# Attention score units of two heads moved among the last chunk's query, key and value products

## What is computed

```python
xn = _layernorm(x, axis=-1)
# attention
qkv = jnp.einsum('bnc,dc->bnd', xn, qkv_w) + qkv_b        # 16 heads of 32
attn = jax.nn.softmax(jnp.einsum('bhqd,bhkd->bhqk', q, k) * scale, axis=-1)
out = jnp.einsum('bhqk,bhkd->bhqd', attn, v)              # then proj_w, proj_b
# feed-forward, two picked experts of each batch
_, idx = jax.lax.top_k(xn[:, 0, :] @ Wr + br, 2)
h = jax.nn.gelu(jnp.einsum('bsd,bkde->bkse', xn, W1[idx]) + b1[idx], approximate=False)
o = jnp.einsum('bkse,bkef->bksf', h, W2[idx]) + b2[idx]   # mean over the two
x = x + attention + mean(o)
```

## Time and profile before

| | us |
|---|---|
| median of 3 runs | 4660.69 |
| lowest and highest run | 4658.37, 4661.96 |
| the profiled execution | 4660.65 |
| its span (first to last instruction) | 4658.9 |
| TensorE busy in the span | 4623.1 |
| VectorE, GpSimd, ScalarE busy | 3206.6, 3176.1, 2392.8 |

### The profile page before, as it was taken

The page is one execution under the profiler, slowest core; times in us unless marked ns, Lnnn a source line. Parts: engine busy times, 40 slices in busy tenths (PEclk is TensorE's granted clock), DMA queues, the critical chain, the costliest instruction groups (busy, mean ns, idle before and its releaser), DMA issues.

```text
span 4658.9 us, 65600 instructions
## 1 busy us (share of the span) xinstructions
PE 4623.1 (99%) x24396; PEld 2958.7 (64%) x24396; DVE 3206.6 (69%) x5313; ACT 2392.8 (51%) x4649; POOL 3176.1 (68%) x1105
## 2 busy tenths in 40 slices
PE   8999999999999999999999999999999999999999
PEld 7888888888755555555555555555555555555567
DVE  5233233333388888888888888888888888888854
ACT  2112121121146666666666666666666666666631
POOL 1121212121268999999999999999999999999910
PEclk9999999999999999999999999999999999999999
DMA  5334353434346666566666666665666666666557
GB/s 176 108 118 138 95 163 93 133 117 135 104 100 135 131 138 135 130 136 135 132 139 133 132 136 134 136 135 128 138 137 132 135 135 132 138 133 136 120 181 259
DMA packets 263425, 629.23 MB, mean 135 GB/s; under 512 B 46788, under 2 KB 83652, under 8 KB 224712
## 3 DMA queue, kind: packets, MB, share of 16 engines
q0 software_dynamic: 36288, 264.26, 27.9%
q1 hardware_dynamic: 226824, 360.85, 27.5%
HBM read 224.96 MB, written 134.74 MB: 77 GB/s over the span
## 4 chain that ended last, share of the span: by engine, by line
PE 62%; POOL 5%; DMA 3%; issue 2%; ACT 1%; DVE 0%; POOLq 0%; DVEq 0%
PE st_ps L1493 20%; PE o_ps L1419 18%; PE mx_ps L1407 18%; POOL p_pair L1121 4%; PE mx_ps L1433 3%; PE st_ps L1441 3%; DMA p_pair<-p_pair 3%; PE mx_ps L1441 1%; ACT p_sb L1197 1%; POOL p_pair L1159 0%; PE mx_ps L1412 0%; POOL o_inv L1115 0%; POOL p_pair L1125 0%; ACT front L1207 0%; DVE y_in L1286 0%
## 5 line engine op out<-in xcount | busy, mean ns | idle before, releaser
L1232 DVE TENSOR_REDUCE unit_max<-mx_ps 128x1 f32<-128x512 f32 x4016 | 2456.4, 682 | 311.1 <-PE mx_ps L1407 309.0
L1197 ACT ACTIVATE p_sb<-st_ps 128x512 f32<-128x512 f32 x4096 | 2063.3, 628 | 860.4 <-PE st_ps L1493 860.3
L1121 POOL TENSOR_TENSOR p_pair<-p_sb 128x2048 f32<-128x2048 f32 x504 | 2433.5, 4875 | 6.7 <-PE mx_ps L1433 3.4
L1419 PE MATMUL o_ps<-p_sb,v_sb 128*32 128x512 f32 x8192 | 986.7, 599 | 0.0
L358 POOL TENSOR_TENSOR h_lo<-h_f,h_hi 128x512 fp32r<-128x512 f32 x128 | 165.3, 1291 | 709.1 <-DVE h_hi L576 709.1
L1419 PEld LDWEIGHTS o_ps<-p_sb,v_sb 128*32 128x32 f32 x8192 | 214.1, 109 | 433.9 <-issue 286.2
L426 ACT ACTIVATE h_f<-rot,b_sb 128x512 f32<-128x512 f32 x128 | 88.1, 689 | 656.0 <-PE rot L627 655.9
L1493 PE MATMUL st_ps<-q_x,k_x 97*128 97x512 f32 x1024 | 401.0, 413 | 1.8 <-ACT p_sb L1197 1.4
L1493 PE MATMUL st_ps<-front 97*128 97x512 f32 x1024 | 399.3, 410 | 1.1 <-ACT p_sb L1197 1.1
L1493 PE MATMUL st_ps<-q_x,front 97*128 97x512 f32 x1024 | 399.1, 410 | 0.0
L1493 PE MATMUL st_ps<-front,k_x 97*128 97x512 f32 x1024 | 398.6, 410 | 0.0
(11 more groups left out here) (124 smaller groups left out, 5922.2 us busy)
## 6 DMA issues: line engine op xcount, KB each, us to landing
p_pair<-p_pair POOLq DMA_DIRECT2D x252, 1024.0 KB, 7.6
xt<-x SPq DMA_DIRECT2D x64, 256.0 KB, 2.7
stage<-w SPq DMA_DIRECT2D x32, 512.0 KB, 4.2
q_hi_d<-qk_hi SPq DMA_DIRECT2D x64, 256.0 KB, 3.1
q_lo_d<-qk_lo SPq DMA_DIRECT2D x64, 256.0 KB, 3.6
k_hi_d<-qk_hi SPq DMA_DIRECT2D x64, 256.0 KB, 2.7
k_lo_d<-qk_lo SPq DMA_DIRECT2D x64, 256.0 KB, 3.4
v_d<-v_out SPq DMA_DIRECT2D x64, 256.0 KB, 2.3
```

Source lines behind the costliest of these rows:

```text
L1121: pool.tensor_tensor(p_pair[:, slot, :, :], p_sb[:, n % SLOTS, :, :], p_sb[:, (n + 1) % SLOTS, :, :], ALU.add).then_inc(pair_done, 1)
L1197: act.activation(p_sb[:, (L * G * KT + n) % SLOTS, h, :], st_ps[bank(g, m)][:, :], ACT.Exp, scale=SCALE).then_inc(exp_done, 1)
L1232: dve.reduce_max(unit_max[:, n // 4, n % 4:n % 4 + 1], mx_ps[UNIT_PLACE[n] % RING][:, :], AX.X).then_inc(bank_read, 1)
L1419: op = pe.matmul(o_ps[rows, :], v_sb[u][:, kt, rows], p_sb[:, (L * G * KT + n) % SLOTS, h, :], start=(kt == 0), stop=(kt == KT - 1))
```

## The change

- The units' order stays, but the first 32 (EARLY_UNITS: heads 0 and 1 of the first group) go in among the last chunk's query, key and value products: none in the first two products, four in each of the products 2 to 7 (one behind each piece c), two in each of the four value products (behind the second and the fourth piece). They use the banks acc[0..3] in turn, so unit n waits for the maximum of unit n - 4, and units 0 to 3 for the residual adds of the chunk before.
- Their queries and keys are loaded by a new `load_early` into the free buffers `xnT_lo[.., 0]`, `xnT_hi[.., 0]` and the old `xt` (`old_xt`): nine DMAs of 256 KB, which SP issues at the start of the last chunk, ahead of that chunk's query and key stores. Unit 0 waits for the three query loads and the three key loads of head 0, unit 16 for the three of head 1.
- VectorE takes the maxima of a product's units behind that product's own step (behind `qk_lo` or the value's bias add).
- In the hidden part 48 units are left: (2, 6) for j = 3 to 7 and (0, 8) for j = 8, of which the last 16 are the second group's. The 16 units behind the last output product are gone. `row_max` is formed behind the hidden step j = 6, its transpose stands at j = 8.
- The first output product of the chunk waits for the maxima of all 32 early units.
- `load_front` still has 18 DMAs, heads 2 and 3 first. At its end TensorE waits for all four heads' keys, which landed long before.

```diff
+        xt_at = next_place(nc)
         xt = sb("xt", [P, TT, C], F32)
+        old_xt = nc.alloc_sbuf_tensor_at("old_xt", [P, N], F32R, offset=xt_at)
...
+        EARLY_HEADS = 2
+        EARLY_UNITS = EARLY_HEADS * UN // 4
-        UNITS = [(0, 0)] * 3 + [(4, 8)] * 5 + [(0, 4)]
+        UNITS_OF = [0] * 2 + [4] * 6 + [2] * 4
         AHEAD_UNITS = 16
+        UNITS = [(0, 0)] * 3 + [(2, 6)] * 5 + [(0, 8)]
+        TURN_AT = 8
...
+        def unit_bank(n):
+            return acc[n % 4] if n < EARLY_UNITS else rot[2 + n % 2]
+        free = NCH % 2
+        early_q = xnT_lo[0:3 * D, free, :, :]
+        early_k = [xnT_hi[0:3 * D, free, :, :].rearrange("p c n -> p (c n)"), old_xt[0:3 * D, :]]
...  (SP)
+                def load_early():
+                    for i in range(2):
+                        sp.wait_ge(qk_st[i], NCH * 4 * 32)
+                    sp.wait_ge(ready["h"], B * NCH * 8 - 8)
+                    sp.wait_ge(ready["t"], B * NCH * TT)
+                    for part, src in enumerate((qh_d, ql_d, qh_d)):
+                        sp.dma_start(early_q[part * D:(part + 1) * D, :, :].bitcast(F32),
+                                     src[0, :, 0:TOK].rearrange("(h d) n -> d h n", d=D)).then_inc(early_ld[2], 16)
+                    for h in range(EARLY_HEADS):
+                        for part, src in enumerate((kh_d, kh_d, kl_d)):
+                            sp.dma_start(early_k[h][part * D:(part + 1) * D, :].bitcast(F32), src[0, h * D:(h + 1) * D, :]).then_inc(early_ld[h], 16)
...
-                        for h in range(2 * qc, 2 * qc + 2):
+                        for h in range(EARLY_HEADS * (1 - qc), EARLY_HEADS * (1 - qc) + 2):
...
                     for i in range(NCH):
                         tok = b * N + i * TOK
+                        if last and i == NCH - 1:
+                            load_early()
                         for m in range(8):
...  (VectorE, behind qk_lo of product m; likewise behind the bias add of value product t)
+                            if last and i == NCH - 1:
+                                units(sum(UNITS_OF[:m]), UNITS_OF[m])
...
                             if end:
                                 units(first_unit(j) + UNITS[j][0], UNITS[j][1])
+                            if end and j == TURN_AT - 2:
+                                dve.wait_ge(front.bank_read, UN)
+                                dve.reduce_max(front.row_max[:, :], front.unit_max[:, :, :], AX.X).then_inc(front.max_done, 1)
...
                             if end:
-                                units(first_unit(8) + t, 1)
-                        if end:
-                            dve.wait_ge(front.bank_read, UN)
-                            dve.reduce_max(front.row_max[:, :], front.unit_max[:, :, :], AX.X).then_inc(front.max_done, 1)
-                            dve.wait_ge(front.max_done, 1)
-                            units(UN, AHEAD_UNITS)
+                                units(first_unit(8) + UNITS[8][1] // TT * t, UNITS[8][1] // TT)
...  (TensorE)
+                    if n == 0:
+                        pe.wait_ge(early_ld[2], 48)
                     if n % (4 * TT) == 0:
-                        pe.wait_ge(front.head_ld[h], 48)
-                    if n < 2:
-                        pe.wait_ge(v_done, B * NCH * TT - 1 + n)
+                        pe.wait_ge(early_ld[h] if early else front.head_ld[h], 48)
+                    if n < 4:
+                        pe.wait_ge(y_added, B * NCH * TT - 2 * TT + n + 1)
+                    elif early:
+                        pe.wait_ge(front.bank_read, n - 3)
...
+                def with_units(out, pairs, u):
+                    n = sum(UNITS_OF[:u])
+                    for c in range(CC):
+                        op = split_product(out, pairs[c:c + 1], c == 0, c == CC - 1)
+                        if c < CC - 1:
+                            for k in range(UNITS_OF[u] * c // CC, UNITS_OF[u] * (c + 1) // CC):
+                                unit(n + k)
+                    for k in range(UNITS_OF[u] * (CC - 1) // CC, UNITS_OF[u]):
+                        unit(n + k)
+                    return op
...
-                    for n in range(UN, UN + 2):
-                        unit(n)
-                    pe.wait_ge(front.max_done, 1)
-                    pe.wait_ge(gelu_done, B * NCH * 8 - 1)
-                    pe.transpose(rot[0][0:4 * TT, 0:P], front.row_max[:, :], ident[:, :]).then_inc(front.rows_ready, 1)
-                    for n in range(UN + 2, UN + AHEAD_UNITS):
-                        unit(n)
+                    for h in range(4):
+                        pe.wait_ge(front.head_ld[h], 48)
```

More of the change, by code:

```diff
@@ L117, in dense_stage @@
         acc = [ctx.enter_context(nc.psum_tensor(f"acc{i}", [P, 512], F32)) for i in range(TT)]
+        early_ld = [sem(f"early_ld{i}") for i in range(3)]
         const_ld, x0_ld, row_ld, zeroed = (sem(n) for n in ("const_ld", "x0_ld", "row_ld", "zeroed"))
@@ L187, in dense_stage @@
         UN = 4 * TT * (N // 512)
-        UNITS = [(0, 0)] * 3 + [(4, 8)] * 5 + [(0, 4)]
+        EARLY_HEADS = 2
+        EARLY_UNITS = EARLY_HEADS * UN // 4
+        UNITS_OF = [0] * 2 + [4] * 6 + [2] * 4
         AHEAD_UNITS = 16
-        assert sum(sum(u) for u in UNITS) == UN
+        UNITS = [(0, 0)] * 3 + [(2, 6)] * 5 + [(0, 8)]
+        TURN_AT = 8
+        assert sum(UNITS_OF) == EARLY_UNITS and sum(sum(u) for u in UNITS) == UN - EARLY_UNITS + AHEAD_UNITS
         def first_unit(j):
-            return sum(sum(u) for u in UNITS[:j])
+            return EARLY_UNITS + sum(sum(u) for u in UNITS[:j])
+        def unit_bank(n):
+            return acc[n % 4] if n < EARLY_UNITS else rot[2 + n % 2]
+        assert first_unit(TURN_AT - 1) == UN
+        free = NCH % 2
+        early_q = xnT_lo[0:3 * D, free, :, :]
+        early_k = [xnT_hi[0:3 * D, free, :, :].rearrange("p c n -> p (c n)"), old_xt[0:3 * D, :]]
         with nc.Block() as block:
@@ L568, in turn @@
                             dve.tensor_tensor(v_out[:, t % 2, :], rot[t % 4][:, :], v_bias[:, :], ALU.add).then_inc(v_done, 1)
+                            if last and i == NCH - 1:
+                                units(sum(UNITS_OF[:8 + t]), UNITS_OF[8 + t])
                         end = last and i == NCH - 1
@@ L663, in last_hidden @@
                                                                                     (xnT_hi[:, s, c, :], xnT_lo[:, s, c, :]))], c == 0, c == CC - 1)
-                                if UNITS[j][0]:
-                                    unit(n + c)
+                                for k in range(UNITS[j][0] * c // CC, UNITS[j][0] * (c + 1) // CC):
+                                    unit(n + k)
                             op.then_inc(ready["h"], 1)
@@ L671, in last_hidden @@
                             pe.wait_ge(h_lo_done, B * NCH * 8 - 8 + k + 1)
+                            if j == TURN_AT:
+                                pe.wait_ge(front.max_done, 1)
+                                pe.wait_ge(gelu_done, B * NCH * 8 - 1)
+                                pe.transpose(rot[0][0:4 * TT, 0:P], front.row_max[:, :], ident[:, :]).then_inc(front.rows_ready, 1)
                             for t in range(TT):
-                                if k == 0:
-                                    pe.wait_ge(y_added, B * NCH * TT - 2 * TT + t + 1)
+                                if k == 0 and t == 0:
+                                    pe.wait_ge(front.bank_read, EARLY_UNITS)
                                 rows = slice(t * P, (t + 1) * P)
@@ L705, in turn @@
                             cols = slice(m * P, (m + 1) * P)
-                            split_product(rot[u % 4][:, :], [((wq_hi[:, c, cols], wq_lo[:, c, cols]), (xnT_hi[:, s, c, :], xnT_lo[:, s, c, :]))
-                                                             for c in range(CC)], True, True).then_inc(ready["qk"], 1)
+                            pairs = [((wq_hi[:, c, cols], wq_lo[:, c, cols]), (xnT_hi[:, s, c, :], xnT_lo[:, s, c, :])) for c in range(CC)]
+                            if last and i == NCH - 1:
+                                with_units(rot[u % 4][:, :], pairs, u).then_inc(ready["qk"], 1)
+                            else:
+                                split_product(rot[u % 4][:, :], pairs, True, True).then_inc(ready["qk"], 1)
                             u += 1
@@ L713, in turn @@
                             rows = slice(t * P, (t + 1) * P)
-                            split_product(rot[u % 4][:, :], [((xnT_hi[:, s, c, rows], xnT_lo[:, s, c, rows]), (wq_hi[:, c, 2 * C:], wq_lo[:, c, 2 * C:]))
-                                                             for c in range(CC)], True, True).then_inc(ready["v"], 1)
+                            pairs = [((xnT_hi[:, s, c, rows], xnT_lo[:, s, c, rows]), (wq_hi[:, c, 2 * C:], wq_lo[:, c, 2 * C:])) for c in range(CC)]
+                            if last and i == NCH - 1:
```

(3 more changed lines are left out.)

14 lines of the change are left out of this document (10 added, 4 removed).

## The result

| | before | after |
|---|---|---|
| median of 7 runs each, us | 4661.5 (4658.37 to 4662.66) | 4676.61 (4674.06 to 4681.41) |
| ratio after to before, 95% interval | | 1.0034 (1.0022 to 1.0046) |
| span of the profiled execution, us | 4658.9 | 4675.5 |

The account below looks back on a forecast made before the run. TensorE, busy 4623.1 of 4658.9 us, was taken as the bound, so only its idle time or needless matmuls could be won. Costs of 29.1 less gains of 17.1 made +12.0, so 4672.7 us; range 4664 to 4683.

Parts of the forecast that it names:

- Cost 1: Last chunk's products: the 32 early-unit matmuls go where TensorE had no gap, 0.233 us each, 7.5 us.
- Cost 2: Unit 0 in product 2: TensorE stands still for the six loads, 11 us, bounds 8.5 and 11.9.
- Cost 3: Behind the load wait: TensorE runs at half clock for 3.4 to 5.7 us, taken as 2 us lost.
- Cost 4: Products 3 to 8: units wait for maxima queued behind VectorE's own step, 8.6 us, bounds 5 and 11.
- Hidden steps: Hidden steps j = 3 to 7: eight units instead of 12 shorten each from 9.34 to 7.75 us, gain 8.0 us.
- The end: End of the dense stage: without trailing units the barrier hangs on the y stores, gain 9.1 us.
- (a): Rival: loads or clock come sooner, stores in time, shorter pacing; 4666 to 4669 us, within 0.2%; chance 0.22.
- (b): Rival: the clock does not recover between the waits from product 3 on, +9.6 us, 4682 us; chance 0.15.
- (c): Rival: early units cost TensorE only their own time, loads there and maxima four ahead; -9.6 us, 4651; chance 0.04.
- (d): Rival: hidden steps do not shorten as reckoned, held by h_lo or two banks; 8.6 us each, 4677; chance 0.07.
- The two do not add: Products 0 to 2: late stores cost under 1 us beside late loads; early loads would lose most of their gain to them.

Follow-up runs that it names:

- e2: Changed kernel, with VectorE taking the maxima of a product's first three units (first one in value products) ahead of its own step: 4666.37 us, ratio 1.0013.
- e8: Changed kernel, nine loads spread behind the last chunk's stores, 16 early units in value products, 16 in hidden steps 0 to 2, maxima first: 4654.99 us, ratio 0.9987.
- e6: Changed kernel, maxima first, early units from product 5 on, loads issued by ScalarE in two parts behind its steps on products 0 and 1: 4663.05 us, ratio 1.0003.
- e7: Changed kernel, maxima first, early units from product 5 on, loads in one block on SP as in the changed kernel: 4666.92 us, ratio 1.0015.
- e5: Kernel before, with the nine early loads added in one block at the changed kernel's place in SP's queue, unused: 4672.62 us, ratio 1.0025.
- e9: Kernel before, with the nine loads added unused, spread in SP's queue behind the last chunk's stores: 4662.25 us, ratio 1.0003.
- e1: Changed kernel, with the nine early loads issued by ScalarE behind its last gelu of the chunk before, not by SP: 4671.77 us, ratio 1.0023.
- e3: Changed kernel, with the loads issued by ScalarE in the chunk before and the maxima taken ahead of VectorE's own step: 4660.99 us, ratio 1.0000.

## Why the prediction was right, and where it was thin

The forecast of 4672.7 us was 3.9 below the median, on the right side and within its range. Its steps, each beside what the profile after shows:

- **Cost 1**, 7.5: the unit matmuls stand 0.233 from their followers at full clock (1232.16 to 1232.39 in the same timeline). Right.
- **Cost 2**, 11, landing at 1222.8 with TensorE at unit 0 at 1211.8: 11.81, at the upper bound (11.9 was written; 1223.6 - 1211.8 is 11.8). From the first load's issue to the landing of head 0's last key load pass 11.4 us, against the 11.2 read off `load_front`. The trace's own transfers of the same size and order were the right measure. The estimate by the Trainium skill's bandwidth figure (DMA: Bandwidth & Descriptors, Specifications), a limit by which six loads take 4.4 us, was off by 7 us; the standstill's window shows 194 GB/s with the DMA engines 0.87 busy.
- **Cost 3**, 2: half clock from 1228.17 to 1231.2, eight matmuls 0.43 apart instead of 0.233, and a first step of 0.56: 1.5 + 0.3 = 1.8 us. Right.
- **Cost 4**, 8.6 from five waits of 1.55 and one of 0.8: products 3 to 7 have one wait each, and a product takes 5.23 us instead of 3.73, so 1.50 each; product 8 has 0.53 of waiting and a restart. 8.3 us. Right, and e2 shows the mechanism by taking it away.
- The four make 29.4; 29.65 were measured.
- **Hidden steps**, 8.0 from steps of 7.75: the five steps took 46.70 us and take 38.35 (from 1286.23 to 1324.58), 7.67 each. The gain is 8.35 us, of which the table has 7.2 ahead of the eighth gelu. Right.
- **The end**, 9.1: from the last hidden step to attention 21.20 us before (from 1299.40) and 13.03 after, a gain of 8.2. The barrier stopped waiting for TensorE as said, and the last product to attention fell from 17.9 to 7.5 (8 was named), 1.4 us more than the 9.1. But the output products of the last step, j = 8, took 5.56 us (1324.58 to 1330.14) instead of 3.26 (1299.40 to 1302.66), since they now have eight units among them instead of four. The prediction put no price on these four units; it had counted what follows the last product and not what the change puts ahead of its end. That 2.3 us is its largest miss, and it was luck that the other one, of 1.4 us, lay the opposite way.
- The gains make 16.5 us where 17.1 was forecast.
- Net: 12.0 predicted, 13.1 in the distances, 15.1 in the medians. Both lie within the medians' interval of 10 to 21.

**The rivals.** (a) did not come: the loads landed at the upper end, and the maxima cost 8.3 us. (b), the clock that does not recover, did not come true: the third window above has clock 1.00 with one wait of 1.2 us in each 5.2 us. The Trainium skill's rule on swinging clocks from cycling through banks (TensorE: Matmul & The Clock Gate, "A second HAM failure mode: psum-queue depth-cycling") does not describe this stretch. (c) did not come, as unit 0 waited 11.81 us for its loads; e8, which comes nearest to its conditions, is 6.7 us under the kernel before (1.9 to 10.3), where (c) had 9.6. (d) fell with the 7.7 us steps.

**Where the reasons were thin.** "The two do not add" was right for this kernel, but it left the second one unpriced. I took the load wait for the cost of the loads and, in e6 and e7, designed around it. e5 shows that the nine issues ahead of the stores cost 9 us in the distances without any unit, and e9 that spreading them costs nothing there and 1.4 us behind it. The 29.65 us up to the first gelu can be split as: about 9 that the block costs without any unit (e5), 4.4 more with units that wait for it (11.8 + 1.8 - 9.2), 8.3 for VectorE's order (e2 took back 7.3), 7.5 for the matmuls. The first two were not shown to add up in one kernel: e7, with the wait at unit 0 cut to 3.3 us, got back 0.55 in this distance.

**What stays open.** Whether e8's remaining wait could be had for nothing by units from product 9 on was not tried. Nor was it found why product 0 begins at times between 1207 and 1211 in kernels that are the same up to there.

## What to carry to other kernels

Before a block of loads goes ahead of stores in a queue, follow the buffers of these stores: which engine waits to write them again, and which waits for that one. Issuing the same block from another engine's queue did not spare the stores here (e1, e6); putting the loads behind the stores, a few at a time, did (e8, e9). A covered cost is not a cost of zero: it can show once the cover is mended, so price it by itself. And where a consumer engine has both a step of its own and reads that free another engine's banks, let it take the reads that are ready first; here that order alone was worth 7 to 10 us.

## What the runs showed of the hardware that was not expected

- With nine loads issued from ScalarE's queue just before, a store of 256 KB on SP's queue took 10.7 us to land instead of 2.1, and a load of x there 11.6 instead of 2.6 (e1).
- The length of a standstill does not tell the length of the half clock behind it: 11.81 us of it were followed by 3.0 us at 1.2 GHz (after), 3.02 us by 5.1 us (e3), 3.19 us by 2.6 us (e1), 1.79 us by at least 3.0 us (e8). Waits of 1.23 us in each 5.23 us (after) and one of 1.51 us (e3) left the clock at 2.4 GHz.
